# Gathering type-sorted node rows by an inverse index, and spreading the self products over more windows, in a two-layer graph network kernel

## The chip, the core and the metric

One NeuronCore of a Trainium2 chip runs the whole program. The metric is device time of one launch in microseconds (us); lower is better. The engines are TensorE (PE; its weight loads are PEld), VectorE (DVE), ScalarE (ACT), GpSimd (POOL) and SyncE (SP, which here only issues DMAs).

## The reference

Two graph layers on 625 nodes with 512 features and 10,000 edges sorted by destination. With h = relu(layernorm(x)):

- Layer 0: `x = x + relu(h[n] @ W_self[type[n]] + b_self[type[n]] + sum over edges e into n of (h[src[e]] @ W_rel[etype[e]] + b_rel[etype[e]]))`, with three node types and three edge types.
- Layer 1, with h computed anew: `q, k, v = h @ W_qkv.T + b_qkv`, eight heads of 64. Each node attends over its incoming edges, duplicates counted, and `x = x + msg @ W_ff.T + b_ff`.

The change touches only the term h[n] @ W_self[type[n]], and the time at which other work of layer 0 is done.

## The kernel before

Nodes are padded to 640, in NT = 5 tiles of 128 rows.

**Adjacency by windows.** The kernel builds, for each source tile and edge type, a matrix of edge counts adjT (source by destination) in fp16. It goes through NW = 20 windows of 32 destinations. For each window DVE makes a `hot_group`: one tensor_tensor `row_hot` (line 840) and six tensor_scalars `key_hot` (line 833). TensorE multiplies the six pairs into one PSUM bank (`first_chunks`, line 1099), and ACT copies the bank to adjT (`store_window`, line 530). The one-hot buffers are two deep: DVE may make the group of window w + 2 only when TensorE has finished window w.

**Self term.** The rows of one node type must be together to be multiplied by one matrix. DVE computes for each node a place in a list of SORTED = 7 tiles of 128 (`sorted_places`, lines 787 to 796), each tile being of one type. ACT makes the normalised rows in0 (line 546). ACT's queue first fills an HBM tensor `sorted_rows` with zeros (line 538); POOL then scatters in0 to it with five indirect DMAs (line 454), and SP reads the seven tiles back in two transfers (line 374) to `hs`, after which it issues the loads of the two other self matrices and of the relation matrices. Each tile then has a `turn` (four transposes, line 1145, ACT copy) and a `self` unit (four fp32 matmuls of 512 columns, which the trace lists as eight, line 1151, ACT copy, then a DMA to `self_rows`). These 14 units, called the pipe, are put by hand after the chunk matmuls of windows 6 to 12 (`pipe_side`, PIPE_AT = 6): one product per window. POOL later gathers `self_sum` by the same places (line 464).

**Aggregation.** After that come `cnt` units (edge counts by type, line 1192) and `z` units (h aggregated by adjacency, ten matmuls each, line 1206), 8 per relation. The first `cnt` and four `z` units cover the first half of the destinations and are put into windows 15 to 19 (`side`, `first_half`); for that, `all_groups` and `all_chunks` (a fallback for windows with more than six chunks, not taken with these inputs) stand at two points. The rest follows in `schedule`, an ordered list that TensorE, ACT and DVE all walk: the products of each relation (`gemm`, line 1260), logarithms of counts for the attention (`m`), then layer 1.

**Work of the other engines in this stretch.** ACT copies in0 to fp16 (`h16_hi`, after windows 1 to 5) and POOL computes the remainder (line 458). ACT copies relation weights for q = 0 and 1 (`weights_hi`, line 521) right after the last pipe unit; POOL computes their remainders (line 446) and the gathers stand between. Each engine executes in its own program order, so an instruction that waits holds all that is behind it.

Of the kernel before, what the change touches and what calls it, by code (L numbers as in the profile page):

```python
# [36 lines left out]
P = 128  # L37
# [5 lines left out]
def gnn_kernel(nc, x_d, src_d, dst_d, etype_d, ntype_d, wrel_d, brel_d, wself_d, bself_d,  # L43
# [17 lines left out]
    PIPE_AT, PIPE_STEP = 6, 1  # L61
# [10 lines left out]
    with ExitStack() as ctx:  # L72
# [33 lines left out]
        place_u = sb("place_u", [P, NT], U32)  # L106
        bounds = sb("bounds", [1, 3, 32], I32)
# [58 lines left out]
        zero_rows = place("zero_rows", o_ss, [P, D], F32)  # L166
# [18 lines left out]
        sorted_d = nc.dram_tensor("sorted_rows", [SP, D], F32, kind="Internal").ap()  # L185
# [26 lines left out]
        s_half = sem("s_half")  # L212
# [4 lines left out]
        s_zero = sem("s_zero")  # L217
        s_scat = sem("s_scat")
        s_hs = [sem("s_hs0"), sem("s_hs1")]
# [45 lines left out]
        side = {w: [] for w in range(NW)}  # L265
        first_half = [("cnt", 0, 0)] + [("z", 0, dt, 0) for dt in range(KD)]
        for n, u in enumerate(first_half):
            side[NW - len(first_half) + n].append(u)

# [5 lines left out]
        schedule = [u for u in [("cnt", 1, 0)] + z_units(0) + z_units(1) if u not in first_half]  # L275
# [17 lines left out]
        ring = [u for w in range(NW) for u in side[w]] + [u for u in schedule if u[0] not in ("gemm", "sum", "ln")]  # L293
# [9 lines left out]
        pipe_side = {w: [] for w in range(NW)}  # L303
        for n, u in enumerate(pipe):
            pipe_side[PIPE_AT + max(n - 1, 0) * PIPE_STEP // 2].append(u)
# [46 lines left out]
        stored = [NW - len(first_half) + 1, NW]  # L352
# [5 lines left out]
        def _(sp):  # L358
# [46 lines left out]
        def _(pool):  # L405
# [20 lines left out]
            nc.gpsimd.memset(zero_rows[:], 0.0).then_inc(s_fill, 1)  # L426
# [75 lines left out]
        def _(act):  # L502
# [25 lines left out]
            def store_window(w):  # L528
# [8 lines left out]
            act.wait_ge(s_x, 48)  # L537
            act.dma_start(sorted_d.rearrange("(t p) d -> p t d", p=P),
                          zero_rows[:].unsqueeze(1).broadcast_to([P, SORTED, D])).then_inc(s_zero, 16)
# [158 lines left out]
        def _(dve):  # L698
# [98 lines left out]

            def tile_types():
# [15 lines left out]
            def biases():  # L814
                dve.wait_ge(s_prep, 7)
# [31 lines left out]
            def all_groups(half):  # L847

                with dve.If(widest > G):
                    dve.wait_ge(s_adj, stored[half])  # L850
                    for w in range(half * NW // 2, (half + 1) * NW // 2):
# [16 lines left out]
                nc.vector.engine_nop().then_inc(s_half, 1)  # L868
# [96 lines left out]
            factors(0, 0, NT)  # L965
            hot_group(1)
            tile_types()
# [4 lines left out]
            for w in range(NW):  # L972
# [3 lines left out]
                if w + 1 in stored:  # L976
                    all_groups(stored.index(w + 1))
# [10 lines left out]
                for u in side[w]:  # L988
                    unit_part(u)
# [70 lines left out]
        def _(pe):  # L1060
# [50 lines left out]
            ins.then_inc(s_prep, 1)  # L1111

            def all_chunks(half):

                with pe.If(widest > G):
                    pe.wait_ge(s_adj, stored[half])
                    for w in range(half * NW // 2, (half + 1) * NW // 2):
# [14 lines left out]
            def adjacency_of(half):  # L1132

                pe.wait_ge(s_adj, NW // 2 * (half + 1))
                pe.wait_ge(s_half, half + 1)

            def pipe_unit(u):
# [4 lines left out]
                if kind == "turn":  # L1142
                    pe.wait_ge(s_hs[0 if t < 2 else 1], 16)
# [17 lines left out]
            def unit(u):  # L1161
# [9 lines left out]
                elif kind == "cnt":  # L1171
# [3 lines left out]
                    adjacency_of(half)  # L1175
                    if half == 0:
                        pe.wait_ge(s_keys, MASKS)
                        pe.wait_ge(s_fill, FILLS)
# [226 lines left out]
```

## Time and profile before

| what | value |
|---|---|
| median of 3 runs | 335.44 us (334.61 to 335.58) |
| profiled execution, its own time | 335.22 us |
| its span | 333.5 us |
| PE busy | 302.0 us, 91% |
| DVE busy | 201.2 us, 60% |
| ACT busy | 143.0 us, 43% |
| POOL busy | 71.7 us, 22% |
| DMA | 22.29 MB moved |

The span is the time between the first and last record of the profile; the own time of the execution is 1.72 us longer. Busy shares are averages over stages that have different limits. In a timeline row the columns are start in us, length in us, engine, line, operation, output<-input, shape and count; a row of several instructions runs from the first start to the last end. In brackets stands how long the engine had been idle and what released it.

### The profile page before, as it was taken

To read this page: it belongs to the slowest core of one execution; us is meant where nothing else is said; L and a number is where in the kernel's file an instruction comes from. 1 tells how busy PE (TensorE), PEld (TensorE's weight loads), DVE (VectorE), ACT (ScalarE), POOL (GpSimd) and SP (SyncE) were. 2 spreads that over 40 slices of the span, in tenths; PEclk is the share of its full clock that TensorE was granted. 3 is DMA by queue.
4 is the path that set the end of the run, shared out by engine and by line. 5 is a ranking of instruction groups with operands and counts; after the bars stand their busy time and mean duration, and the time that the engine had idled before them with its cause. 6 is when DMAs were issued, how large, how long until landed. Compare 5 with 4: busy or idle time off the path is not lost.

```text
span 333.5 us, 5488 instructions
## 1 busy us (share of the span) xinstructions
PE 302.0 (91%) x2006; PEld 228.6 (69%) x2006; DVE 201.2 (60%) x471; ACT 143.0 (43%) x282; POOL 71.7 (22%) x97
## 2 busy tenths in 40 slices
PE   2757699996699999999999999999799999999994
PEld 2512344442356778868788789999688888888883
DVE  5999944557794324434446962784976556565721
ACT  1155213236032332253342451677876466565721
POOL 6059500005840004470001330320001002020202
PEclk9999789998599999999999999999999999999999
DMA  5852894110740000003520000000000000000000
GB/s 173 281 186 100 267 392 154 38 64 33 253 152 13 2 1 3 2 2 128 149 103 2 0 0 3 0 2 1 0 2 0 34 2 2 32 2 33 1 33 28
DMA packets 10970, 22.29 MB, mean 67 GB/s; under 512 B 950, under 2 KB 966, under 8 KB 10938
## 3 DMA queue, kind: packets, MB, share of 16 engines
q1 hardware_dynamic: 8772, 16.80, 14.5%
q0 software_dynamic: 800, 2.62, 2.2%
q10 hardware_dynamic: 1366, 2.45, 2.1%
q8 instruction: 20, 0.33, 0.4%
q14 instruction: 12, 0.10, 0.1%
HBM read 15.60 MB, written 6.26 MB: 66 GB/s over the span
## 4 chain that ended last, share of the span: by engine, by line
PE 78%; DVE 14%; issue 2%; ACT 2%; DMA 2%; POOL 0%; DVEq 0%
PE banks L1260 13%; PE banks L1246 8%; PE banks L1206 8%; PE banks L1151 8%; PE banks L1349 7%; PE banks L1335 7%; PE banks L1324 7%; DVE key_hot L833 6%; PE banks L1099 6%; PE banks L1369 5%; DVE row_hot L840 3%; PE banks L1192 2%; DMA raw<-in_L_gnn_W_qkv_dram 2%; PE banks L1359 2%; PE banks L1236 1%
## 5 line engine op out<-in xcount | busy, mean ns | idle before, releaser
L1099 PE MATMUL banks<-key_hot,row_hot 128*128 128x480 f16 x120 | 35.8, 438 | 14.7 <-DVE key_hot L833 12.3
L1019 DVE CUSTOM_DVE_ANT_0 s_sb<-banks,mask_add 128x640 f32<-128x640 f32 x40 | 32.6, 822 | 22.2 <-PE banks L1324 22.1
L833 DVE TENSOR_SCALAR key_hot<-iota,picked 128x480 f16<-128x480 f16 x120 | 41.2, 410 | 0.0
L673 ACT ACTIVATE p_sb<-s_sb,neg_max 128x640 f32<-128x640 f32 x40 | 32.9, 823 | 17.3 <-DVE neg_max L1019 17.3
L1099 PEld LDWEIGHTS banks<-key_hot,row_hot 128*128 128x128 f16 x120 | 12.7, 108 | 36.8 <-DVE key_hot L833 15.7
L1206 PE MATMUL banks<-adjT,h 128*128 128x320 f16 x240 | 33.8, 299 | 0.6 <-DVE zT_even L892 0.6
L840 DVE TENSOR_TENSOR row_hot<-iota,picked_row 128x768 f16<-128x768 f16 x20 | 21.9, 1097 | 18.9 <-PE banks L1099 18.9
L1206 PEld LDWEIGHTS banks<-adjT,h 128*128 128x128 f16 x240 | 23.2, 98 | 10.4 <-DVE zT_even L892 1.2
L1335 PE MATMUL banks<-ident,p_sb 128*128 128x128 f32 x200 | 29.6, 275 | 0.2 <-ACT pT L680 0.2
L1260 PE MATMUL banks<-w_hl,zT_even 128*128 128x512 f32 x120 | 29.2, 394 | 0.0
L497 POOL TENSOR_TENSOR msgT<-msg_f,msgT 128x128 fp32r<-128x128 f32 x20 | 8.6, 460 | 95.7 <-ACT msgT L694 95.7
L1324 PE MATMUL banks<-k_hi,q_st 128*128 128x320 f32 x80 | 27.1, 348 | 2.0 <-DVE neg_max L1019 2.0
L1246 PE MATMUL banks<-h2T,wqkvT 128*128 128x320 f32 x192 | 28.3, 309 | 0.0
L1246 PEld LDWEIGHTS banks<-h2T,wqkvT 128*128 128x128 f32 x192 | 28.2, 188 | 0.1
L530 ACT ACTIVATE adjT<-banks 128x480 f16<-128x480 f32 x20 | 11.3, 570 | 37.2 <-PE banks L1099 37.1
L1151 PE MATMUL banks<-w_self,hsT 128*128 x56 | 26.7, 622 | 0.0
L1349 PE MATMUL banks<-pT,v_sb 128*64 128x128 f32 x400 | 26.0, 277 | 0.0
L1335 PEld LDWEIGHTS banks<-ident,p_sb 128*128 128x128 f32 x200 | 23.5, 141 | 3.0 <-issue 1.9
L1260 PEld LDWEIGHTS banks<-w_hl,zT_even 128*128 128x128 f32 x120 | 22.3, 188 | 4.4
L1349 PEld LDWEIGHTS banks<-pT,v_sb 128*64 128x64 f32 x400 | 21.5, 137 | 4.0 <-issue 3.8
L1324 PE MATMUL banks<-k_lo,q_st 128*128 128x320 f32 x80 | 24.0, 309 | 0.0
L446 POOL TENSOR_TENSOR w_hl<-raw,w_hl 128x512 fp32r<-128x512 f32 x12 | 15.0, 1284 | 41.5 <-ACT w_hl L521 41.5
(176 smaller groups left out, 473.3 us busy)
## 6 DMA issues: line engine op xcount, KB each, us to landing
w_self<-in_L_gnn_W_self_dram SPq DMA_DIRECT2D x3, 1024.0 KB, 9.4
raw<-in_L_gnn_W_rel_dram SPq DMA_DIRECT2D x3, 1024.0 KB, 14.6
raw<-in_L_gnn_W_qkv_dram SPq DMA_DIRECT2D x3, 1024.0 KB, 5.2
sorted_rows<-zero_rows ACTq DMA_DIRECT2D x1, 1792.0 KB, 10.9
self_rows<-hs SPq DMA_DIRECT2D x7, 256.0 KB, 2.0
hs<-sorted_rows SPq DMA_DIRECT2D x1, 1280.0 KB, 7.2
xs<-in_x_dram SPq DMA_DIRECT2D x1, 1024.0 KB
raw<-in_L_gnn_W_ff_dram SPq DMA_DIRECT2D x1, 1024.0 KB, 5.4
```

What stands on the lines that cost most here:

```text
L673: nc.scalar.activation(p_sb[:, n % NPR, :], s_sb[:, n % NS, :], ACT.Exp, scale=-1.0, bias=neg_max[:, it, h:h + 1], accum_out=denom[:, it, ...
L833: return nc.vector.tensor_scalar(to_key, iota[:], float(KEYS * w), key, ALU.add, ALU.is_equal)
L840: nc.vector.tensor_tensor(row_hot[:, par], iota[:, 0:P].unsqueeze(1).broadcast_to([P, G, P]), picked_row[:, w * G:(w + 1) * G].unsqueeze(2 ...
L1019: nc.vector.tensor_tensor_reduce(s_sb[:, n % NS, :].rearrange("p (a j) -> p a j", a=2), banks[:, c:c + 2, 0:HALF], mask_add[:, it, :].rear ...
L1099: mm(banks[:, w % 2, 0:KEYS], row_hot[:, w % 2, k, :], key_hot[:, w % 2, k, :], start=(k == 0), stop=True, skip_group_check=True).then_inc ...
L1151: ins = mm(pipe_bank(u), hsT[:, t % 4, kt, :], w_self[:, bass.ds(offsets[t] + kt * D, D)], start=(kt == 0), stop=(kt == KD - 1))
L1206: ins = mm(b[:, 0:HALF], h16[:, p, jt, feats], adj[:, jt, r, cols], start=(start and n == 0), stop=(stop and n == len(pick) - 1), skip_gro ...
L1246: ins = mm(b[:, 0:HALF], wqkvT[:, pw, kt, o:o + P], h2T[:, ph, kt, half * HALF:(half + 1) * HALF], start=(n == 0), stop=(n == 3 * KD - 1))
L1260: ins = mm(to, lhs[:, pl, kt, it * P:(it + 1) * P], weights[:, pw, kt, c0:c0 + cn], start=(start and n == 0), stop=(n == 3 * KD - 1), skip ...
L1324: ins = mm(banks[:, 2 * (n % 2) + half, 0:HALF], q_st[:, h, it * P:(it + 1) * P], k[:, h, cols], start=(p == 0), stop=(p == 1))
L1335: ins = nc.tensor.transpose(banks[:, 5 + n % 2, i * P:(i + 1) * P], p_sb[:, h % NPR, jt * P:(jt + 1) * P], ident[:])
L1349: ins = mm(banks[64 * hh:64 * hh + 64, 4, a * P:(a + 1) * P], v_sb[:, jt, h * DK:(h + 1) * DK], pT[:, s, :], start=(jt == 0), stop=(jt == ...
```

## The change

Three things change. (1) The zero fill, the scatter and the read back go. SP stores the five tiles of in0 in node order (`rows`), between the loads of self matrices 1 and 2. DVE makes five 128x896 one-hots of the places, TensorE multiplies them with the node numbers in 35 matmuls of one column, DVE turns the result into `node_u`, and POOL gathers the seven tiles into `hs`, with a semaphore for each. (2) The pipe starts at window 3, and product t stands at window 3 + 16t // 7, so at windows 3, 5, 7, 9, 12, 14 and 16. The first `cnt` and four `z` units leave the windows and go to the front of `schedule`; the fallback stands once, after window 19. (3) `h16_hi` moves to windows 9 to 13, and `weights_hi(0)` and `weights_hi(1)` go behind the windows and in front of relation 1's z units.

```diff
-    PIPE_AT, PIPE_STEP = 6, 1
+    PIPE_FROM, PIPE_OVER = 3, 16
-        schedule = [u for u in [("cnt", 1, 0)] + z_units(0) + z_units(1) if u not in first_half]
+        schedule = [("cnt", 0, 0), ("cnt", 1, 0)] + z_units(0) + z_units(1)
-        pipe = [("turn", 0), ("turn", 1)]
+        pipe_side = {w: [] for w in range(NW)}
+        pipe_side[PIPE_FROM] += [("turn", 0), ("turn", 1)]
         for t in range(SORTED):
-            pipe += [("self", t)] + [("turn", t + 2)] * (t + 2 < SORTED)
+            pipe_side[PIPE_FROM + t * PIPE_OVER // SORTED] += [("self", t)] + [("turn", t + 2)] * (t + 2 < SORTED)
...
             self_weights(0)
-            sp.wait_ge(s_scat, 16 * NT)
-            for half, (t0, t1) in enumerate(((0, 2), (2, SORTED))):
-                sp.dma_start(hs[:, t0:t1, :], sorted_d[t0 * P:t1 * P, :].rearrange("(t p) d -> p t d", p=P)
-                             ).then_inc(s_hs[half], 16)
             self_weights(1)
+            for it in range(NT):
+                sp.wait_ge(s_y0, it + 1)
+                sp.dma_start(rows_d[it * P:(it + 1) * P, :], in0[:, it, :]).then_inc(s_rows, 16)
             self_weights(2)
...
-            pool.wait_ge(s_place, 1)
-            pool.wait_ge(s_zero, 16)
-            for it in range(NT):
-                pool.wait_ge(s_y0, it + 1)
-                nc.gpsimd.indirect_dma_start(sorted_d, bass.IndirectOffsetOnAxis(ap=place_u[:, it:it + 1], axis=0),
-                                             in0[:, it, :], None).then_inc(s_scat, 16)
+            nc.gpsimd.iota(slot_iota[:], [[1, SP]], base=0, channel_multiplier=0,
+                           allow_small_or_imprecise_dtypes=True).then_inc(s_fill, 1)
+            pool.wait_ge(s_node, 1)
+            pool.wait_ge(s_rows, 16 * NT)
+            for t in range(SORTED):
+                nc.gpsimd.indirect_dma_start(hs[:, t, :], None, rows_d,
+                                             bass.IndirectOffsetOnAxis(ap=node_u[:, t:t + 1], axis=0)).then_inc(s_hs[t], 16)
...
-            act.dma_start(sorted_d.rearrange("(t p) d -> p t d", p=P),
-                          zero_rows[:].unsqueeze(1).broadcast_to([P, SORTED, D])).then_inc(s_zero, 16)
...
-                        if u == pipe[-1]:
-                            weights_hi(0)
-                            weights_hi(1)
-                    for u in side[w - 1]:
-                        unit_part(u)
                     store_window(w)
-                if 1 <= w < 1 + NT:
-                    h16_hi(w - 1)
-            for u in side[NW - 1]:
-                unit_part(u)
+                if 9 <= w < 9 + NT:
+                    h16_hi(w - 9)
+            weights_hi(0)
             for u in schedule:
-                if u == ("z", 2, 0, 0):
-                    weights_hi(2)
+                if u in (("z", 1, 0, 0), ("z", 2, 0, 0)):
+                    weights_hi(u[1])
...
+            def place_one_hots():
+                dve.wait_ge(s_fill, FILLS + 1)
+                for it in range(NT):
+                    nc.vector.tensor_scalar(place_hot[:, it, :], slot_iota[:], place_n[:, it:it + 1], None,
+                                            ALU.is_equal).then_inc(s_inv, 1)
+
+            def nodes_of_slots():
+                dve.wait_ge(s_prep, 7)
+                nodes = banks[:, 4, 460:460 + SORTED]
+                nc.vector.tensor_scalar(node_u[:], nodes, -1.0, 0.0, ALU.add, ALU.max).then_inc(s_node, 1)
...
             factors(0, 0, NT)
+            place_one_hots()
             hot_group(1)
+            nodes_of_slots()
             tile_types()
...
+            pe.wait_ge(s_inv, NT)
+            for t in range(SORTED):
+                for it in range(NT):
+                    ins = mm(banks[:, 4, 460 + t:461 + t], place_hot[:, it, t * P:(t + 1) * P], node_id[:, it:it + 1],
+                             start=(t == 0 and it == 0), stop=True, skip_group_check=True)
+            ins.then_inc(s_prep, 1)
...
-                    pe.wait_ge(s_hs[0 if t < 2 else 1], 16)
+                    pe.wait_ge(s_hs[t], 16)
```

The 35 matmuls stand on TensorE after the rank matmuls of line 1108 and before the chunks of window 1. TensorE also waits for s_node at window 2.

## Rows read from the trace of the kernel before

**Rows 1.** Busy time by stretch: us, each engine's busy (instructions), granted clock, DMA share, GB/s
```profile
0.00:38.00 38.00, 20.92 (x69) 10.13 (x69) 33.40 (x104) 11.83 (x20) 21.71 (x39) 0.98 0.56 187
38.00:77.00 39.00, 38.90 (x128) 19.20 (x129) 21.01 (x64) 11.93 (x22) 0.00 (x0) 0.93 0.46 172
77.00:103.00 26.00, 19.98 (x97) 10.33 (x95) 21.79 (x40) 8.56 (x12) 15.64 (x13) 0.80 0.40 144
```

**Rows 2.** Timeline, TensorE and DVE in the windows of the self products
```profile
66.34 1.38 PE L1099 MATMUL banks<-key_hot,row_hot 128*128 128x480 f16 x6
...
71.43 1.38 PE L1099 MATMUL banks<-key_hot,row_hot 128*128 128x480 f16 x6
...
72.85 0.96 DVE L840 TENSOR_TENSOR row_hot<-iota,picked_row 128x768 f16<-128x768 f16 x1 [2.60 <-PE banks L1099]
...
76.08 2.59 PE L1099 MATMUL banks<-key_hot,row_hot 128*128 128x480 f16 x12
```

**Rows 3.** Timeline, the windows after the last product
```profile
78.37 5.66 DVE L833 TENSOR_SCALAR key_hot<-iota,picked 128x480 f16<-128x480 f16 x6
78.75 5.13 POOL L446 TENSOR_TENSOR w_hl<-raw,w_hl 128x512 fp32r<-128x512 f32 x4 [40.88 <-ACT w_hl L521]
...
87.16 4.21 PE L1192 MATMUL banks<-adjT,sel 128*70 128x320 f16 x15
...
92.72 3.89 DVE L840 TENSOR_TENSOR row_hot<-iota,picked_row 128x768 f16<-128x768 f16 x1 [0.30 <-PE banks L1099]
```

**Rows 4.** Busy time by stretch, the lowest clock in those windows
```profile
84.00:88.00 4.00, 1.72 (x8) 0.99 (x9) 4.00 (x12) 0.57 (x1) 3.35 (x3) 0.50 0.60 207
```

**Rows 5.** Timeline, the second cnt unit and twelve z units
```profile
103.20 2.20 PE L1192 MATMUL banks<-adjT,sel 128*70 128x320 f16 x15
105.24 16.46 PE L1206 MATMUL banks<-adjT,h 128*128 128x320 f16 x120
```

**Rows 6.** Timeline, ACT and DVE before window 2
```profile
17.91 2.91 ACT L546 ACTIVATE in<-xs,shift,rstd 128x512 f32<-128x512 f32 x4
...
19.46 0.21 DVE L799 TENSOR_SCALAR tile_off<-tile_iota,type_base 1x8 f32<-1x8 f32 x1
...
21.32 0.93 DVE L840 TENSOR_TENSOR row_hot<-iota,picked_row 128x768 f16<-128x768 f16 x1
...
23.71 0.94 DVE L840 TENSOR_TENSOR row_hot<-iota,picked_row 128x768 f16<-128x768 f16 x1
```

**Rows 7.** Timeline, small matmuls with a new stationary operand each
```profile
13.02 2.25 PEld L1108 LDWEIGHTS banks<-type_mask,ones 128*128 128x128 f32 x10
...
124.54 1.01 PE L1223 MATMUL banks<-ident,adjT 128*128 128x128 f16 x15
```

**Rows 8.** Lines 454 and 464: ns min/median/max, first and last start; landing of 464
```profile
L454 POOL DMA_INDIRECT sorted_rows<-in,place_u x5: 960/1175/5195, 20.2 to 31.1; - x5
...
L464 POOL DMA_INDIRECT self_sum<-self_rows,place_u x5: 946/960/1716, 84.0 to 89.9; - x5
...
DMA to landing us min/median/max: 4.1/4.4/6.0
```

**Rows 9.** The longest scatter, in the POOL timeline
```profile
24.21 5.20 POOL L454 DMA_INDIRECT sorted_rows<-in,place_u  x1 [0.30 <-issue]
```

**Rows 10.** Timeline, POOL and DVE at window 6, and the first self product
```profile
32.06 5.82 POOL L458 TENSOR_TENSOR h<-in,h 128x512 f16<-128x512 f32 x5
...
32.18 6.09 DVE L833 TENSOR_SCALAR key_hot<-iota,picked 128x480 f16<-128x480 f16 x6
...
40.79 5.10 PE L1151 MATMUL banks<-w_self,hsT 128*128 x8
```

**Rows 11.** Timeline, POOL weight remainders beside a z unit's DVE part
```profile
144.57 4.95 POOL L446 TENSOR_TENSOR w_hl<-raw,w_hl 128x512 fp32r<-128x512 f32 x4 [0.57 <-ACT w_hl L521]
147.58 0.49 DVE L892 TENSOR_TENSOR zT_even<-banks,zT_even 128x320 fp32r<-128x320 f32 x1 [1.37 <-ACT zT_even L573]
```

**Rows 12.** DMA issues: KB each, median us to landing
```profile
self_rows<-hs SPq DMA_DIRECT2D x7, 256.0 KB, 2.0
```

More of the change, by code:

```diff
@@ L106, in gnn_kernel @@
         place_u = sb("place_u", [P, NT], U32)
+        node_u = sb("node_u", [P, SORTED], U32)
         bounds = sb("bounds", [1, 3, 32], I32)
@@ L165, in gnn_kernel @@
         place_n = place("place_n", o_r4 + 61472, [P, NT], F32)
-        zero_rows = place("zero_rows", o_ss, [P, D], F32)
+        slot_iota = place("slot_iota", o_r4 + 61760, [P, SP], F16)
+        node_id = place("node_id", o_r4 + 63552, [P, NT], F16)
+        place_hot = place("place_hot", o_z0 + 10240, [P, NT, SP], F16)
         mlog = place("mlog", o_r4 + 43136, [P, 2, 512], F32)
@@ L183, in gnn_kernel @@
         msgT = place("msgT", o_r4 + 27136, [P, 2, 2, KD, P], F32R)
-        sorted_d = nc.dram_tensor("sorted_rows", [SP, D], F32, kind="Internal").ap()
+        rows_d = nc.dram_tensor("rows", [NP, D], F32, kind="Internal").ap()
         self_d = nc.dram_tensor("self_rows", [SP, D], F32, kind="Internal").ap()
@@ L216, in gnn_kernel @@
         s_wself = [sem(f"s_wself{t}") for t in range(T)]
-        s_zero = sem("s_zero")
-        s_scat = sem("s_scat")
-        s_hs = [sem("s_hs0"), sem("s_hs1")]
+        s_inv = sem("s_inv")
+        s_node = sem("s_node")
+        s_rows = sem("s_rows")
+        s_hs = [sem(f"s_hs{t}") for t in range(SORTED)]
         s_pipe = sem("s_pipe")
@@ L262, in gnn_kernel @@
         s_out = [sem("s_out0"), sem("s_out1")]
[L265 to L268, printed above, removed]
         def z_units(r):
             return [("z", r, dt, half) for dt in range(KD) for half in range(2)]
-        schedule = [u for u in [("cnt", 1, 0)] + z_units(0) + z_units(1) if u not in first_half]
+        schedule = [("cnt", 0, 0), ("cnt", 1, 0)] + z_units(0) + z_units(1)
         for it in range(NT):
@@ L292, in gnn_kernel @@
         schedule += [("q", a, half) for a in range(KD) for half in range(2)]
-        ring = [u for w in range(NW) for u in side[w]] + [u for u in schedule if u[0] not in ("gemm", "sum", "ln")]
+        ring = [u for u in schedule if u[0] not in ("gemm", "sum", "ln")]
         number = {u: n for n, u in enumerate(ring)}
@@ L297, in bank @@
             return banks[:, 5 + number[u] % 3, :]
-        pipe = [("turn", 0), ("turn", 1)]
+        pipe_side = {w: [] for w in range(NW)}
+        pipe_side[PIPE_FROM] += [("turn", 0), ("turn", 1)]
         for t in range(SORTED):
-            pipe += [("self", t)] + [("turn", t + 2)] * (t + 2 < SORTED)
+            pipe_side[PIPE_FROM + t * PIPE_OVER // SORTED] += [("self", t)] + [("turn", t + 2)] * (t + 2 < SORTED)
+        pipe = [u for w in range(NW) for u in pipe_side[w]]
         pipe_no = {u: n for n, u in enumerate(pipe)}
-        pipe_side = {w: [] for w in range(NW)}
-        for n, u in enumerate(pipe):
-            pipe_side[PIPE_AT + max(n - 1, 0) * PIPE_STEP // 2].append(u)
         def pipe_bank(u):
@@ L845, in hot_group, with all_groups @@
                     key_one_hot(key_hot[:, par, k, :], picked[:, 1, n:n + 1], w).then_inc(s_hot, 1)
-            def all_groups(half):
+            def all_groups():
                 with dve.If(widest > G):
-                    dve.wait_ge(s_adj, stored[half])
-                    for w in range(half * NW // 2, (half + 1) * NW // 2):
+                    dve.wait_ge(s_adj, NW)
+                    for w in range(NW):
                         lo = dve.value_load(bounds[0:1, 0, w:w + 1], min_val=0, max_val=EC)
@@ L987, in _ @@
                                             bhl[BG:BG + R + T, :].bitcast(F32), ALU.subtract).then_inc(s_blo, 1)
-                for u in side[w]:
-                    unit_part(u)
+            all_groups()
             for u in schedule:
@@ L1111, in _, with all_chunks @@
             ins.then_inc(s_prep, 1)
-            def all_chunks(half):
+            pe.wait_ge(s_inv, NT)
[4 more added lines that the diff above has]
+            ins.then_inc(s_prep, 1)
+            def all_chunks():
                 with pe.If(widest > G):
-                    pe.wait_ge(s_adj, stored[half])
-                    for w in range(half * NW // 2, (half + 1) * NW // 2):
+                    pe.wait_ge(s_adj, NW)
+                    for w in range(NW):
                         count = pe.value_load(bounds[0:1, 2, w:w + 1], min_val=1, max_val=EC)
@@ L1174, in unit @@
                     cols = slice(half * HALF, (half + 1) * HALF)
-                    adjacency_of(half)
                     if half == 0:
+                        pe.wait_ge(s_adj, NW)
+                        pe.wait_ge(s_whole, 1)
                         pe.wait_ge(s_keys, MASKS)
@@ L1274, in _ @@
                         skip_runtime_bounds_check_because="the vector engine worked them out")
-                if w + 1 in stored:
-                    all_chunks(stored.index(w + 1))
                 for u in pipe_side[w]:
                     pipe_unit(u)
-                for u in side[w]:
-                    unit(u)
                 if w == 6:
@@ L1284, in _ @@
                                         ).then_inc(s_prep, 1)
+            all_chunks()
             for u in schedule:
```

18 lines of the change are left out of this document (6 added, 12 removed).

## The prediction, made before the changed kernel was run

> **What bounds the kernel now.** I read the busy time by stretch first. Up to 38 us DVE is busy 33.4 of 38 us and TensorE only 20.9; from 38 to 77 us TensorE is busy all the time (38.9 of 39) and DVE 21.0; from 77 to 103 us neither is full, 20.0 and 21.8 of 26 us [rows 1]. So the 20 windows are bound by DVE, then by TensorE, then by turns by each. The timelines say why. In the middle part a window lasts 5.09 us (chunk matmuls start at 66.34 and 71.43), and DVE stands idle for 2.60 us of it until TensorE is done with a buffer [rows 2]. A DVE group alone needs 2.39 us (row_hot starts at 21.32 and 23.71) [rows 6]. Six chunk matmuls alone add 1.22 us on TensorE (12 of them last 2.59 us and six 1.38), and a window with a product but no turn lasts 4.65 us (71.43 to 76.08) [rows 2]. Hence a product costs 4.65 - 1.22 = 3.43 us and its turn 5.09 - 4.65 = 0.44 us.
>
> Twenty groups are 47.8 us of DVE work, and the chunks, products and turns are 24.4 + 24.0 + 3.1 = 51.5 us of TensorE work at full speed. Run beside each other they would need little over 50 us. In the trace they go from about 18 us (group 1) to 103 us, with 9 to 10 us of cnt and z units among them. The losses besides the unequal mixing are four. Six key_hots took 6.09 us where POOL's subtractions ran at 32 us [rows 10]; in a free group 2.39 us less row_hot's 0.93 is left for them, about 1.6 us with the overlap of neighbours [rows 6]. Six took 5.66 us and one row_hot 3.89 us beside POOL's weight remainders [rows 3]. The first cnt unit took 4.21 us at a granted clock of about 0.5, the lower level of 1.2 GHz, against 2.20 us for the second [rows 3 to 5]. These are 4.5 + 4.0 + 2.9 + 2.0 = 13.4 us, almost all on the path.
>
> **The change, as a new walk through the windows.** The terms below are not differences but a clock time for each step, since many of them overlap.
>
> *The index.* DVE's five 128x896 one-hots are not in the trace. A key_hot of 480 elements adds about 0.27 us (1.6 / 6) [rows 6]. No more than in proportion, 0.50 us, and no less than the same, 0.27: 1.3 to 2.5 us in all. I take 2.0 (0.4 each), since a fixed part must be in 0.27. Group 1, which started at 17.07 (21.32 less 1.86 of small operations, less 2.39) [rows 6], ends at 21.5. TensorE's 35 one-column matmuls run beside it, from 19.1. Their price is that of loading a new 128x128 operand: 0.07 us in the 15 fp16 matmuls of 1.01 us at full clock, 0.225 us in fp32 [rows 7], so 2.4 to 7.9 us. I take twice the pitch that lies between 0.85 and 1.01 us for 15 (0.057), for the lower clock: 0.113 x 35 = 4.0 us, to 23.1. DVE waits for them in front of tile_types, with groups 2 and later queued behind the wait. So node_u is ready at 23.3, and the small operations of 1.86 us [rows 6] put group 2 at 25.2 instead of 21.32: **+3.9 us** at once, visible on the path. Group 3 ends at 30.0, 4 at 32.4, 5 at 34.8.
>
> *Stores and gathers.* in0 is complete at 20.8 [rows 6]; SP has nothing before the stores but two weight loads issued by 9 us, and a 256 KB store lands in 2.0 us [rows 12], so `rows` is there at about 23.3, beside node_u. This edit takes no time of its own: the index ends as late. POOL then issues seven gathers. Undisturbed one takes 0.96 us and 0.3 us between [rows 9], median landing 4.4 us; under DVE's groups five scatters went from 20.2 to 32.0, so 2.36 us each [rows 8], the longest 5.20 [rows 9]. The bounds for a gather are thus 1.26 and 5.5 us. The first falls beside DVE's small operations and is issued at 24.7. With 2.4 us for the second it is issued at 27.4, with 5.5 at 30.2; landing 4.4 us gives 31.8 to 34.6. I take 33.6. The third lands before 38 and is needed only after the first product.
>
> *A rule about this.* Rows 9 show a scatter held for 5.20 us while DVE made groups back to back, and rows 8 that others got through in about 1 us. The Trainium skill ("SBUF — State Buffer", section "SBUF: two separate sides") says that a DVE instruction in a two-port mode locks GpSimd out, so that it cannot write the descriptors of its DMAs. Taken strictly, gathers advance only when DVE stands still, which would be after group 5. The rows support it only in part; what it would cost is worked out as rival B.
>
> *Window 3.* The chunks of windows 2 and 3 at the lower level end at about 31.4; turn 0 follows to 32.2, turn 1 waits for its gather and ends at 34.0, and the first product takes 5.10 us as it did before at the lower level [rows 10]: 39.1, and with turn 2 39.5. Window 4's chunks end at 40.8 and, as group 5 is long ready, window 5's at 42.0.
>
> *Steady windows.* A window with a product and one without are 5.09 + 1.22 = 6.31 us of TensorE against 4.78 us of DVE. So window 7 ends at 48.3 and 9 at 54.6. From 9 to 12 there are three windows: DVE's two groups after window 10 give 5.09 + 2.39 + 0.3 = 7.8 us. In this stretch POOL's five h16 remainders now run, 5.82 / 5 = 1.16 us each, one per window [rows 10]. Spread out, most fall into DVE's slack; I charge 1.0 here and 0.7 in 12 to 14, between 0 and 4.5 (what they cost before). Window 12 ends at 63.4 and 14 at 70.4 (6.31 + 0.7). The products of windows 14 and 16 have no turn behind them: 16 ends at 76.3 (4.65 + 1.22) and 17 at 80.9. Then DVE decides, with group 19 made after that: 83.6.
>
> *After the windows.* Both cnt units and all z units follow: 0.3 + 2.4 + 2.2 us, and 16 z at 16.46 / 12 = 1.37 us, 21.9 us [rows 5]. This is 26.8 us, to **110.4 us**. Before, the z units ended at 121.7 (105.24 + 16.46) [rows 5]. The gain is 11.3 us. weights_hi(0) runs on ACT beside the cnt units, where ACT has no copies to make; weights_hi(1) delays an ACT copy by some 1 us, within the three banks of the ring. POOL's remainders now lie beside z units; their DVE part took 0.49 us beside just such POOL work [rows 11], so I charge nothing. Without that cover, four POOL operations would hold DVE for 4 us each time, as in rows 3. Behind this point the order of work is unchanged.
>
> **Sum.** 335.2 - 11.3 = 323.9 us against the profiled execution's own time, which lies 0.2 us under the median shown, so I keep 323.9.
>
> **Rivals.**
> A. *Nothing delays window 3.* The second gather lands in time and TensorE is at its upper level, since it has been nearly continuously busy from 19 us. Then turn 1 saves 1.4 us and the product 1.7, and with 1 us less for the index it is about 4 us better: 319.9 us. For it: the granted clock up to 38 us is 0.98 on average [rows 1]. Against: the first product took 5.10 us all the same [rows 10].
> B. *The gathers starve.* DVE goes back to back from 25.2 to 34.8, as it did when one scatter took 5.20 us. Gathers 1 and 2 are issued after 35 us, gather 1 lands at about 40.5, and window 4 ends near 47.8 instead of 40.8: 7 us less gain, 330.9 us. Against it: half of the scatters amid groups took no more than 1.18 us [rows 8]. By the rule of the Trainium skill's page this is what happens.
> C. *Slower: TensorE's clock does not hold in the thinned windows.* Where products stood in every window the clock was at its full level; where DVE paced the windows it fell, to 0.5 at 84 to 88 us [rows 4]. Now DVE paces windows 10 to 12 and 16 to 19. If the clock falls there and stays low through the cnt units, then work worth 16.8 us from 12 to 16 (three products, a turn and five sets of chunks) doubles, of which TensorE's own waits hide about 4, so that 13 us are added: about 336.9 us. It turns the result to slower from the point where more than 11.3 us of full-speed work runs at the lower level. Against it: the idle times now are 1 to 2 us at a time, and windows with products have no gap.
> D. *No change.* B's 7 us and a lower level at one place alone, for some 4 us of work, give 11 together: 335 us, within 0.3% (1 us, about what a measurement of this kernel can tell from no change).
>
> **Chances.** Forecast 0.50 (its own range 321.9 to 326.5), A 0.16, B 0.24, C 0.05, D and its like 0.05. The predicted time is the forecast's, 323.9. The range goes from 319.7, A, to 331.5, B with half a microsecond more. Faster by over 0.3%: 0.90; same 0.04; slower 0.06.
>
> **What would show it.** Right: group 2 starts near 25 us; the 35 matmuls last 4 us; the first product starts near 34 and lasts 5.1 us; products at windows 5, 7, 9 leave DVE idle for 1.5 us per pair; no key_hot group of over 5 us; window 19's chunks end at 83 to 85; z ends near 110. Wrong: gathers of over 4 us each before the first product (B), or lower-level rows after 45 us (C). If the windows end at 84 but the time doesn't fall by 11 us, something in layer 1 moved, which I excluded.

## The result, and the profile after

The changed kernel takes 330.83 us (329.81 to 330.99, 4 runs) beside 335.51 us before; the ratio is 0.9855 (95% interval 0.9824 to 0.9887). So it is faster, by 4.7 us and not by 11.3. Its profiled execution took 330.99 us (span 329.2), against 335.22. The z units of relations 0 and 1 end at 117.4 us instead of 121.7 [rows 5], and 4.2 of these 4.3 us are left at the end: behind this point nothing changed, as forecast. All that has to be explained lies in the windows and, for 1.4 us, in the cnt and z units right behind them.

The index first. Timeline of DVE and of TensorE in the changed kernel, before window 2:

```profile
21.12 0.15 DVE L797 TENSOR_SCALAR node_u<-banks 128x7 uint32<-128x7 f32 x1
...
23.05 0.94 DVE L841 TENSOR_TENSOR row_hot<-iota,picked_row 128x768 f16<-128x768 f16 x1
```

```profile
18.86 1.09 PE L1115 MATMUL banks<-node_id,place_hot 128*128 128x1 f16 x35 [3.66 <-DVE place_hot L790]
19.98 2.58 PE L1099 MATMUL banks<-key_hot,row_hot 128*128 128x480 f16 x6
```

The 35 matmuls last 1.09 us, and node_u is there at 21.3, not 23.3; group 2 starts at 23.05 instead of 21.32 [rows 6]. But the index is no longer what ends last. The chain of waits, in order of time (start, us, what):

```profile
20.69 4.22 DMA rows<-in
...
25.77 8.74 DMA hs<-rows,node_u
...
34.56 1.11 PE banks L1146 x4
...
36.93 5.10 PE banks L1152 x8
...
57.77 3.43 PE banks L1152 x8
...
63.85 2.83 DVE key_hot L834 x4
...
67.61 5.20 PE banks L1152 x8
...
89.19 0.58 ACT adjT L528
```

The first two rows are the stores of `rows` (the last is issued at 20.69 and landed at 24.9) and the first gather with its transfer (8.74 us). TensorE waits for them in front of turn 0 until 34.5. The row at 63.85 is DVE held at six key_hots, and the one after it a product that took 5.20 us where 3.43 is normal. DMA issues by line, with KB each and median us to landing, say the same of the first part:

```profile
rows<-in SPq DMA_DIRECT2D x5, 256.0 KB, 4.0
...
hs<-rows,node_u POOLq DMA_INDIRECT x7, 6.4
```

A store lands in 4.0 us where rows 12 had 2.0, a gather in 6.4 where rows 8 had 4.4. DVE's timeline shows what follows for it:

```profile
43.72 0.96 DVE L841 TENSOR_TENSOR row_hot<-iota,picked_row 128x768 f16<-128x768 f16 x1 [10.68 <-PE banks L1099]
...
63.76 3.41 DVE L834 TENSOR_SCALAR key_hot<-iota,picked 128x480 f16<-128x480 f16 x6
...
68.79 2.58 DVE L834 TENSOR_SCALAR key_hot<-iota,picked 128x480 f16<-128x480 f16 x6
...
75.38 2.51 DVE L834 TENSOR_SCALAR key_hot<-iota,picked 128x480 f16<-128x480 f16 x6
```

DVE is idle for 10.68 us, since both buffers are full while TensorE stands at window 3; later three of its groups are held by POOL's h16 remainders (key_hots of 3.41, 2.58 and 2.51 us instead of 1.60). The busy time by stretch (columns as in rows 1) has the low granted clock of the product at window 12, which lasts 5.37 us in the timeline:

```profile
68.00:72.00 4.00, 4.00 (x7) 1.58 (x6) 4.00 (x8) 0.74 (x2) 1.15 (x1) 0.64 0.02 6
```

The first product lasts 5.31 us in the timeline, but the granted clock of 36.7 to 42 us is given as 1.00. That it ran in part at the lower level is read from its length (3.60 us for the others), here and in the runs below, and not from the clock column.

### The profile page after: what moved, and what is told of

Same layout as the page of the kernel before. It is cut to its first block, busy times and chain, and to the rows that moved or that the text cites. A ratio compares the mean times of both kernels' runs of the same rounds, so it can differ in the third digit from the quotient of the medians.

```text
span 329.2 us, 5541 instructions
## 1 busy us (share of the span) xinstructions
PE 300.2 (91%) x2041; PEld 229.0 (70%) x2041; DVE 195.8 (59%) x477; ACT 143.1 (43%) x282; POOL 70.5 (21%) x100
## 4 chain that ended last, share of the span: by engine, by line
PE 80%; DVE 7%; DMA 6%; ACT 3%; issue 2%; POOL 1%; ACTq 0%; DVEq 0%; POOLq 0%
PE banks L1261 13%; PE banks L1247 9%; PE banks L1207 9%; PE banks L1152 8%; PE banks L1348 7%; PE banks L1334 7%; PE banks L1323 7%; PE banks L1099 6%; PE banks L1368 5%; DMA hs<-rows,node_u 3%; DMA raw<-in_L_gnn_W_qkv_dram 2%; PE banks L1358 2%; PE banks L1237 1%; PE banks L1194 1%; PE banks L1146 1%
## 5 line engine op out<-in xcount | busy, mean ns | idle before, releaser
L1099 PE MATMUL banks<-key_hot,row_hot 128*128 128x480 f16 x120 | 32.0, 413 | 5.5 <-DVE key_hot L834 5.4
L834 DVE TENSOR_SCALAR key_hot<-iota,picked 128x480 f16<-128x480 f16 x120 | 36.0, 366 | 0.0
L841 DVE TENSOR_TENSOR row_hot<-iota,picked_row 128x768 f16<-128x768 f16 x20 | 19.9, 994 | 15.9 <-PE banks L1099 15.7
L1152 PE MATMUL banks<-w_self,hsT 128*128 x56 | 28.7, 660 | 0.0
L528 ACT ACTIVATE adjT<-banks 128x480 f16<-128x480 f32 x20 | 11.4, 570 | 26.2 <-PE banks L1099 25.8
L669 ACT ACTIVATE pT<-banks 128x512 f32<-128x512 f32 x25 | 14.6, 586 | 14.5 <-PE banks L1334 14.5
```

What stands on the lines that cost most here:

```text
L834: return nc.vector.tensor_scalar(to_key, iota[:], float(KEYS * w), key, ALU.add, ALU.is_equal)
L841: nc.vector.tensor_tensor(row_hot[:, par], iota[:, 0:P].unsqueeze(1).broadcast_to([P, G, P]), picked_row[:, w * G:(w + 1) * G].unsqueeze(2 ...
L1099: mm(banks[:, w % 2, 0:KEYS], row_hot[:, w % 2, k, :], key_hot[:, w % 2, k, :], start=(k == 0), stop=True, skip_group_check=True).then_inc ...
L1152: ins = mm(pipe_bank(u), hsT[:, t % 4, kt, :], w_self[:, bass.ds(offsets[t] + kt * D, D)], start=(kt == 0), stop=(kt == KD - 1))
```

## The experiments

All times are medians; ratios are to the kernel before, on the same chip. The changed kernel gave 330.8 and, in a later set, 329.5 us, so a gain against it is known to about 1.3 us. Differences to the changed kernel are given against both sets where that matters.

| run | us | ratio (95%) |
|---|---|---|
| changed kernel | 330.8 | 0.9855 (0.9824 to 0.9887) |
| the same again (e11) | 329.5 | 0.9845 (0.9819 to 0.9871) |
| e1 weight loads after the third tile | 327.2 | 0.9770 (0.9744 to 0.9796) |
| e2 h16 copies at windows 1 to 3 | 327.0 | 0.9762 (0.9719 to 0.9805) |
| e9 bias broadcasts first | 328.4 | 0.9825 (0.9789 to 0.9861) |
| e12 these three together | 323.0 | 0.9665 (0.9628 to 0.9702) |
| e7 products from window 4 | 326.5 | 0.9770 (0.9740 to 0.9801) |
| e3 products from window 5 | 321.4 | 0.9591 (0.9566 to 0.9615) |
| e5 from window 5, one in each window | 329.2 | 0.9860 (0.9820 to 0.9900) |
| e8 e3 with e1, e9 and spaced h16 copies | 319.8 | 0.9554 (0.9531 to 0.9577) |
| e4 part 1 of the change alone | 332.5 | 0.9924 (0.9902 to 0.9947) |
| e6 parts 2 and 3 alone | 328.7 | 324.1 to 333.1, no ratio given |
| e6b the same again | 330.8 | 325.6 to 332.7, no ratio given |
| e10 e3 with scatters | 321.6 | 319.5 to 327.4, no ratio given |
| e14 e3 with scatters and a pause of DVE | 321.2 | 0.9595 (0.9571 to 0.9619) |

What one kernel's executions differ in is seen in the changed kernel itself. The profile of e11 (327.45 us) has nearly the same wait of TensorE (4.15 us) and POOL's remainders at the same place, but both slow products are shorter than in the profile above (5.31 and 5.37 us):

```profile
36.70 4.13 PE L1152 MATMUL banks<-w_self,hsT 128*128 x8
...
66.24 3.68 PE L1152 MATMUL banks<-w_self,hsT 128*128 x8
```

These are 2.9 of the 3.5 us between the two executions. What decides it, no run here shows.

**e1_loads_late.** The late tiles: whose fault?

```diff
+            sp.wait_ge(s_hs[2], 16)
             self_weights(2)
```

> SP waits for the third gathered tile before it issues the loads of self matrix 2 and of relation matrices 0 and 1 (3 MB). Theory T (the missing gain has two causes: gathered rows that land late behind these loads, and POOL's h16 remainders in windows paced by DVE): landing of the gathers falls from 6.4 us to about 4.4, the first product starts at 34 to 35 us instead of 36.7, the time falls by about 2 us to 329. Rival P (the gathers are late because DVE's groups hold up their issue): issue and landing stay, first product at 36.7 us, time 331 as after.

Its DMA issues, and TensorE's timeline:

```profile
hs<-rows,node_u POOLq DMA_INDIRECT x7, 4.5
```

```profile
32.18 1.97 PE L1147 MATMUL banks<-ident,hs 128*128 128x128 f32 x8 [1.79 <-DMA hs<-rows,node_u]
34.18 4.62 PE L1153 MATMUL banks<-w_self,hsT 128*128 x8
```

Landing falls to 4.5 us, the issues keep their lengths (2.16, 2.09, 1.46, then 0.95 us), and TensorE's wait falls from 4.21 to 1.79 us. Theory T holds for this cause, P does not for the landing. The gain is 3.7 us (2.3 against the later set) where 2 were expected; in the profiles the first product starts 2.5 us earlier. The rest of the difference to the first profile (4.62 instead of 5.31 us for this product, 3.68 instead of 5.37 for the one at window 12) came in e11 without this edit.

**e2_h16_early.** POOL's remainders.

```diff
-                if 9 <= w < 9 + NT:
-                    h16_hi(w - 9)
+                for it in ((), (0, 1), (2, 3), (4,))[w] if w < 4 else ():
+                    h16_hi(it)
```

> ACT's fp16 copies of in0 go to windows 1 to 3 instead of 9 to 13, so that POOL's remainders follow the gathers at 37 to 43 us, where DVE is idle. Theory T: no key_hot group over 2 us in windows 9 to 14, the product of window 12 back from 5.37 to 3.6 us, windows 9 to 14 about 3 to 4 us shorter, time 327. Rival C (spread windows let TensorE's clock fall by themselves): the clock falls in windows 10 to 12 all the same and the time falls by less than 1.5 us.

Timeline of POOL, and of TensorE at window 12:

```profile
37.21 5.60 POOL L456 TENSOR_TENSOR h<-in,h 128x512 f16<-128x512 f32 x5
```

```profile
63.57 1.56 PE L1099 MATMUL banks<-key_hot,row_hot 128*128 128x480 f16 x6 [0.18 <-DVE key_hot L834]
64.97 3.68 PE L1152 MATMUL banks<-w_self,hsT 128*128 x8
```

The five remainders lie in DVE's idle time, no group is held, and the product of window 12 takes 3.68 us: 3.8 us gained (2.5 against the later set), near T's 3 to 4. Windows thinned out by themselves did not let the clock fall. In e1 and in e11 the same remainders held DVE just as long and the product of window 12 took 3.68 us as well. So the clock's fall does not have to follow, and of the 3.8 us the 1.7 of this product are not shown to be the edit's.

**e9_bias_first.** Why a store lands late.

```diff
+            act.dma_start(bv_rows[:], bqkv_d[2 * D:3 * D].partition_broadcast(P)).then_inc(s_bias, 16)
+            act.dma_start(bff_rows[:], bff_d.partition_broadcast(P)).then_inc(s_bias, 16)
             def weights_hi(q):
...
                 rows0(it)
-            act.dma_start(bv_rows[:], bqkv_d[2 * D:3 * D].partition_broadcast(P)).then_inc(s_bias, 16)
-            act.dma_start(bff_rows[:], bff_d.partition_broadcast(P)).then_inc(s_bias, 16)
```

> The two broadcast loads bv_rows and bff_rows (256 KB each) go from 17 us, just ahead of the stores of rows, to the start of ACT's queue. Theory B (these two make a store land in 4.1 us instead of 2.0): stores land in under 3 us, POOL's first gather is issued at about 24 us instead of 25.8, the first product starts 1 to 2 us earlier, time 329.5. Rival W (the stores wait for the weight loads or for nothing that moves): landing 4 us, gather at 25.8, time 331.

```profile
rows<-in SPq DMA_DIRECT2D x5, 256.0 KB, 2.1
...
hs<-rows,node_u POOLq DMA_INDIRECT x7, 6.8
```

```profile
23.93 1.12 POOL L452 DMA_INDIRECT hs<-rows,node_u  x1 [17.19 <-DMA rows<-in]
...
27.63 0.95 POOL L452 DMA_INDIRECT hs<-rows,node_u  x1 [0.30 <-issue]
```

A store lands in 2.1 us and the first gather is issued at 23.93 instead of 25.77. Theory B holds. The first product starts 1.7 us earlier (35.01), but lasts 5.54 us. The gathers land in 6.8 us; that they do so because they are now issued nearer to the 3 MB of weights is argued from e1, not tested here. The time is 2.4 us lower (1.1 against the later set).

**e12_three_terms.** The three edits together, products still from window 3.

> The changed kernel, products from window 3, with the edits of e1_loads_late, e2_h16_early and e9_bias_first together, which restore three sizes that the forecast assumed (a store lands in 2.0 us, a gather in 4.4, POOL's remainders cost little). Theory T3 (the forecast failed by these sizes and not in its walk): first product at 32 to 33 us, window 19's chunks at about 83, time 323 to 325, the forecast's 323.9. Rival K (window 3 is a bad place in itself, since TensorE has no chunk work behind it while DVE fills both buffers): 326 or more, as the best of the three alone.

```profile
32.25 3.66 PE L1154 MATMUL banks<-w_self,hsT 128*128 x8
...
86.86 21.90 PE L1209 MATMUL banks<-adjT,h 128*128 128x320 f16 x160
```

The kernel takes 323.0 us; the forecast was 323.9, and rival K's 326 is out. But the steps of the walk did not come out with the sum. Window 5 ends at 38.8 us, 3.2 before the forecast's 42.0: the first product starts at 32.25 instead of 34.0 and lasts 3.66 us instead of 5.10. The z units start at 86.9, only 1.6 before the forecast's 88.5. One thing lost in between is in DVE's timeline:

```profile
37.60 4.78 DVE L843 TENSOR_TENSOR row_hot<-iota,picked_row 128x768 f16<-128x768 f16 x1 [4.55 <-PE banks L1101]
```

TensorE now frees the buffer earlier, so POOL's remainders (35.95 to 41.56) no longer lie in DVE's idle time; this row_hot takes 4.78 us instead of 0.95, and the product of window 7 starts about 1.7 us late. So the third size was moved, not restored, and part of the agreement with 323.9 is luck.

**e3_from5, e7_from4.** Not to wait at all.

```diff
-    PIPE_FROM, PIPE_OVER = 3, 16
+    PIPE_FROM, PIPE_OVER = 5, 14
```

(e7: `4, 15`.)

> Products at windows 5, 7, 9, 11, 13, 15 and 17 instead of 3 to 16. Theory T: TensorE goes on with the chunks of windows 4 and 5 while the tiles are in flight, its 4.2 us wait in front of the first turn goes, and the time falls by 2 to 3 us, to 328. Rival P: without an idle DVE the gathers are issued at over 4 us each, the first product starts after 41 us, the time is 331 or more.

> Products at windows 4, 6, 8, 10, 12, 14 and 16. Theory T2: the chunks of window 4 end at about 33.5 us, turn 0 waits for 1 us and turn 1 for another, and the time lies between after and e3_from5, nearer to the latter: 324 us. Rival C2 (the difference of 9.4 us between after and e3_from5 is mostly TensorE's clock, which fell in the wait): with the wait cut to 2 us the clock stays up and all of it comes back, 321.5 us.

TensorE's timeline in e3, then in e7:

```profile
27.81 6.32 PE L1099 MATMUL banks<-key_hot,row_hot 128*128 128x480 f16 x18 [0.84 <-DVE key_hot L834]
...
35.53 0.66 PE L1146 MATMUL banks<-ident,hs 128*128 128x128 f32 x4 [0.97 <-DMA hs<-rows,node_u]
36.02 3.60 PE L1152 MATMUL banks<-w_self,hsT 128*128 x8
...
85.78 21.90 PE L1207 MATMUL banks<-adjT,h 128*128 128x320 f16 x160
```

```profile
33.29 0.66 PE L1146 MATMUL banks<-ident,hs 128*128 128x128 f32 x4 [0.54 <-DMA hs<-rows,node_u]
35.74 0.90 PE L1146 MATMUL banks<-ident,hs 128*128 128x128 f32 x4 [1.80 <-DMA hs<-rows,node_u]
36.44 5.09 PE L1152 MATMUL banks<-w_self,hsT 128*128 x8
```

In e3 the first product starts at 36.0 us, only 0.7 us before that of the changed kernel, but with two more windows done, and it lasts 3.60 us instead of 5.31. The z units of e3 start at 85.8 instead of 95.0. The gain is 9.4 us (8.1 against the later set) and not the expected 3. Time in which TensorE waits at window 3 is lost on DVE as well, whose two buffers are full; in e3 DVE made groups 6 and 7 meanwhile.

The profiles allow a split of the 9.7 us by the end of the z units. With window 5, the first product and its turn done, e3 is 5.0 us ahead (39.9 against 44.9): 2.4 for the chunks of two windows, 1.7 for the product's length, the rest for the earlier start. Another 3.7 arise up to window 19 and 1.0 behind it. There e3 differs in more than its start: its products stand in every second window up to 17, none of its products took over 3.68 us, and POOL's remainders, which stretched two groups of key_hots to 3.41 us, held TensorE up by only about 0.7 us. So not all of the 9.4 us is the wait at window 3.

Rival P is out: e3's gathers took 2.19, 2.09 and 1.43 us and then 0.94 to 1.23, though DVE worked on. At window 4 the waits are 0.54 and 1.80 us, but the first product still takes 5.09 us. C2's 321.5 us is refuted: with the waits cut to 2.3 us the product is as slow as before. By the lengths above, the clock is 1.7 us of the difference at the first product and up to 1.7 at window 12, so not most of 9.4. 326.5 us is less near to e3 than I expected.

**e5_from5_dense.** What the spreading itself is worth (`5, 7`).

> Products start at window 5, as in e3_from5, but stand in every window, 5 to 11, instead of every second one. Theory T2 (the start at window 3 cost most of the missing gain, the spreading is worth as much as DVE's idle time in windows bound by TensorE): windows 5 to 11 take 5.1 us each with 2.6 us of DVE idle, then windows 12 to 19 are paced by DVE at 2.4 us with nothing else on TensorE, so 20 - 6 = about 7 us are lost against e3_from5 and the time is 328. Rival N (only the later start matters): 321 to 322 as e3_from5.

```profile
35.93 3.60 PE L1152 MATMUL banks<-w_self,hsT 128*128 x8
...
73.80 0.38 PE L1099 MATMUL banks<-key_hot,row_hot 128*128 128x480 f16 x1 [0.75 <-DVE key_hot L834]
...
83.85 1.56 PE L1099 MATMUL banks<-key_hot,row_hot 128*128 128x480 f16 x6 [0.83 <-DVE key_hot L834]
86.24 1.56 PE L1099 MATMUL banks<-key_hot,row_hot 128*128 128x480 f16 x6 [0.83 <-DVE key_hot L834]
```

Started as e3, it is 7.8 us slower, T2's 7 us and not N's nothing. After the last product TensorE waits for DVE: within a window whose key_hots POOL's remainders hold (0.75 us at 73.80), and for 0.83 us in front of each of the last ones, so that a window lasts 2.39 us (83.85 to 86.24). From 76 to 80 us the granted clock was 0.57, which is part of the 7.8. So starting late enough and spreading are both needed.

**e4_gather_only.** Part 1 alone, in the kernel before.

> The kernel before with part 1 of the change alone (stores, index, seven gathers); products in windows 6 to 12, half units, h16 copies and weight copies stay where they were. Theory T: the tiles are there at about 36 us instead of 38, POOL's h16 remainders fall into the windows bound by TensorE instead of window 6, so the first product starts at 37 to 38 instead of 40.8 and the time is 332 to 333. Rival S (the gain is all in the spreading): the later group 2 eats what the gathers save, time 335.

```profile
37.75 3.70 PE L1173 MATMUL banks<-w_self,hsT 128*128 x8 [0.47 <-ACT hsT L603]
```

```profile
36.99 7.42 DVE L847 TENSOR_SCALAR key_hot<-iota,picked 128x480 f16<-128x480 f16 x6
...
75.84 5.66 DVE L847 TENSOR_SCALAR key_hot<-iota,picked 128x480 f16<-128x480 f16 x6
```

The first product starts at 37.8 instead of 40.8 and lasts 3.70 us instead of 5.10: 2.5 us gained, as expected. But POOL's remainders still stop DVE, now in group 7 (six key_hots in 7.42 us), and the weights stop it at 75.8 as in rows 3.

**e6_scatter_spread, e6b, e10, e14: what the gathers are worth.** These keep the zero fill, the scatters and the read back, with parts 2 and 3 of the change.

> Parts 2 and 3 of the change alone: products from window 3, spread, with the zero fill, scatter and read back of the kernel before. Theory T2: the tiles land at 38 us or later, so that TensorE waits at window 3 for 7 us or more instead of 4.2; part 3 takes POOL's remainders out of window 6 and the weights out of the windows; 332 to 334 us. Rival S (parts 2 and 3 carry the gain by themselves): 331 as after.

> The kernel of e6_scatter_spread again, since its four executions lay between 324.1 and 333.1 us. If they spread alike again, the time hangs on how long the scatters are held (one took 6.85 us in that profile); T2 expects a median of 329 to 333, not under that of e11_change_again by more than 2 us; rival S expects it 2 us under it.

> The changed kernel itself, beside the others: 330.8 us, for the comparison with e6b_scatter_spread on one chip.

> e3_from5 with the zero fill, scatter and read back in place of stores, index and gathers; so against e3_from5 it shows what part 1 is worth when the products start at window 5. Theory T2: the tiles land at 38.5 us, window 5 ends at 33, TensorE waits 5 us, the clock falls, and the time is 326 to 327, so part 1 is worth about 5 us. Rival S: 322, part 1 is worth nothing as it costs DVE 2 us for the index.

The executions of these kernels lie far apart: 324.1, 328.2, 329.2 and 333.1 us for e6, 325.6 to 332.7 in six executions of e6b, and 319.5, 319.9, 323.2 and 327.4 us for e10. By its median e6b (330.8) is not under e11 (329.5) on the same chip, so rival S, which wanted it 2 us lower, is out. The profiles caught both ends. POOL's timeline in e6 (333.1 us), e6b (325.6) and e10 (327.4):

```profile
22.58 6.85 POOL L447 DMA_INDIRECT sorted_rows<-in,place_u  x1 [0.31 <-issue]
```

```profile
21.18 0.97 POOL L447 DMA_INDIRECT sorted_rows<-in,place_u  x1 [0.30 <-ACT in L539]
22.46 0.96 POOL L447 DMA_INDIRECT sorted_rows<-in,place_u  x1 [0.30 <-issue]
```

```profile
22.53 7.07 POOL L447 DMA_INDIRECT sorted_rows<-in,place_u  x1 [0.30 <-issue]
```

And what TensorE waited for in e6 and in e6b, in front of the first turn:

```profile
38.80 1.97 PE L1124 MATMUL banks<-ident,hs 128*128 128x128 f32 x8 [10.19 <-DMA hs<-sorted_rows]
```

```profile
31.60 1.97 PE L1124 MATMUL banks<-ident,hs 128*128 128x128 f32 x8 [2.23 <-DMA hs<-sorted_rows]
```

One scatter held for 6.85 us goes with tiles at 38.8 us, none held with tiles at 31.6. It ends at 29.4 us, as the held one of rows 9 did (24.21 + 5.20), soon after DVE's first wait for a buffer, which in the trace of before came at 28.6 us. In e6b DVE's groups 2 and 3 took 0.15 to 0.2 us longer each and the scatters went through; in e6 it ran without a break. Which of the two is the cause, the profiles don't show. For this the last kernel makes DVE stand still while the scatters are issued:

```diff
                 if w == 2:
+                    dve.wait_ge(s_pause, 32)
...
-                                             in0[:, it, :], None).then_inc(s_scat, 16)
+                                             in0[:, it, :], None).then_inc(s_pause if it < 2 else s_scat, 16)
```

> e10_scatter_from5 with DVE waiting in front of group 2 until the first two scatters have landed, so that DVE stands still for about 3 us while POOL issues the second to fourth scatter. Theory H (a scatter is held by DVE's groups made back to back until DVE's first pause): the executions come within 1.5 us of each other, no scatter takes over 2.5 us in the profile, and the time is 321 to 324 us, since the pause costs DVE about 3 us. Rival Q (the hold comes from the DMA queues, where 2.8 MB of zeros and weights are under way until 19 us): scatters of 5 us or more again, and executions 5 us or more apart.

```profile
23.87 0.96 DVE L831 TENSOR_TENSOR row_hot<-iota,picked_row 128x768 f16<-128x768 f16 x1 [2.24 <-DMA sorted_rows<-in,place_u]
```

```profile
22.40 0.96 POOL L449 DMA_INDIRECT sorted_rows<-in,place_u  x1 [0.30 <-issue]
...
24.92 1.00 POOL L449 DMA_INDIRECT sorted_rows<-in,place_u  x1 [0.30 <-issue]
```

No scatter is held, and four executions lie between 321.03 and 321.68 us. All three marks of theory H came out, and none of rival Q's. The last scatter (24.92) went through beside running groups, so a busy DVE alone does not hold one. With products from window 5, scatters and a pause cost the same as stores, index and gathers (321.4), and e10's two fastest executions, without a pause, 1.5 to 1.9 us less: there part 1 is worth evenness, not time. In the kernel before, it was worth 2.5 us (e4). At window 3 the tiles of unheld scatters came 3 us before the gathered ones. My expectation for e10 (326 to 327, part 1 worth 5 us) took a held scatter for the rule, as that one trace of before had shown it.

**e8_best.** e3 with e1 and e9, and one h16 copy in windows 6, 8, 10, 12 and 14.

> Four edits together: products from window 5 in every second window, the weight loads after the third gathered tile, the two bias broadcasts at the start of ACT's queue, and one h16 copy in each window without a product from 6 to 14. Theory T2: what is left in e3_from5 is 1 us of wait at the second tile and 0.7 us around POOL's remainders, so 320 us (319.5 to 320.7). Rival O (the edits take each other's place, since the first product of e3_from5 already starts when window 5 ends): 321.4, no difference.

```profile
35.10 3.69 PE L1154 MATMUL banks<-w_self,hsT 128*128 x8 [0.47 <-issue]
...
84.12 21.90 PE L1209 MATMUL banks<-adjT,h 128*128 128x320 f16 x160
```

319.75 us, 4.5% under the kernel before and 1.6 us under e3; T2 holds. From 33.6 us TensorE has hardly a gap up to the end of the windows. e12 with nearly the same edits, but products from window 3, takes 3.3 us more. With window 5, the first product and its turn done, the two stand level (39.2 us here, 38.8 in e12), so a start at window 3 costs nothing there once the tiles come early. e12 loses behind that point: at window 7, as shown above, and at windows 12 and 19, where the chunks of three windows in a row (10 to 12, 17 to 19) let DVE set the pace.

## Why the prediction was wrong

The direction was right, and so was where the gain lies: the 4.3 us are there when the z units end, no group was held by weight remainders, layer 1 did not move. The size was off by more than a factor of two, because three steps of the walk were mis-sized: the landing of the stores, the landing of the gathers, and what POOL's remainders cost. Forecast and trace, in us from the start:

| step | forecast | measured |
|---|---|---|
| node_u ready | 23.3 | 21.3 |
| first gather's issue starts | 23.4 (24.7 less 1.26) | 25.8 |
| first product starts, its length | 34.0, 5.10 | 36.7, 5.31 |
| window 5 ends | 42.0 | 44.9 |
| window 9 ends | 54.6 | 57.8 |
| window 12, 14 ends | 63.4, 70.4 | 67.6, 75.7 |
| window 19 ends | 83.6 | 89.2 |
| z units | 88.5 to 110.4 | 95.0 to 117.4 |

- *"This edit takes no time of its own: the index ends as late"* failed, twice over. The index came 2.0 us early (its matmuls were bounded at 2.4 us from below by matmuls of 128 columns, and one-column matmuls took 1.09), and the stores 2 us late. The 2.0 us of rows 12 is a median of seven stores, five of them issued after 55 us, where the queues moved about 52 GB/s, little more than these stores themselves; the stores of `rows` had two broadcasts just ahead (e9).
- *Landing 4.4 us, "I take 33.6"* failed likewise: 6.4 us, since SP issues 3 MB of weights in front of the gathers (e1). I had listed SP's queue and looked only at what stands before the stores. Together 2.9 us by window 5, and 0.3 more by window 9.
- *The remainders, "I charge 1.0 here and 0.7"*: 1.0 too little between windows 9 and 12, and another 1.1 to window 14, where the clock fell for one product (5.37 us). e2 gives back 3.8 us (2.5 against the later set).
- *After the windows*: window 19 itself ended another 0.3 us late. Then 0.71 us for ACT's copy of window 19 and small gaps between the two cnt units, 1.0 us by the start of the z units. Within them 0.4 us were lost to an ACT copy that came about 1.9 us late at 103.9 us, for a reason that the trace does not show; in e11, the same kernel, the 160 matmuls run through in 21.90 us. weights_hi(1) was hidden, as forecast.

These are 2.9 + 0.3 + 1.0 + 1.1 + 0.3 + 1.0 + 0.4 = 7.0 us, the difference at 117.4. They are those of one execution at the slow end; in e11's profile the z units end at 114.1, 3.7 us behind the forecast, mostly since the two products at 36.7 and 66.2 us were shorter. e12 supports that these sizes failed: with the stores and gathers early and the remainders elsewhere it takes 323.0 us against 323.9. It does not prove the walk, whose steps it passes by up to 3.2 us before it loses part of that again. What the walk did not ask is whether window 3 and the uneven spacing were good choices: it took a wait of TensorE at its length, though DVE with full buffers pays it again, and it let DVE set the pace at windows 12 and 19, behind the chunks of three windows in a row. e3, which changes both, is 9.4 us faster; with tiles and broadcasts early as well, the difference is 3.3 us (e12 against e8).

Rival B's number, 330.9, came out, but not by its mechanism: gathers were issued in 2.3 us, not held until DVE's pause, and e3 with a busy DVE issued them alike. So it is luck that the time lies within the stated range, whose upper part stood there for B. Rival C's clock fall came for a single product, and not in e11. D and A did not occur.

## What to carry to other kernels

Price a DMA by a row with the same company, not by the nearest row of the same size: list what every queue issues in the 5 us before and after it. Put work that waits for a transfer behind the point where the transfer has surely landed, above all when the waiting engine feeds a partner with two buffers, since both then stop. And when a kernel's executions spread, as those of e6, e10 and, by 3.5 us, the changed kernel do, ask for the profile at either end before pricing what one of them showed.

## What was unexpected of the hardware

- A 256 KB store landed in 4.0 us with two 256 KB broadcasts issued just ahead on another queue, and in 2.1 us without them.
- An indirect DMA's issue takes 0.95 us alone. Under back-to-back DVE groups, the first two gathers took 2.1 to 2.3 us and ended just after the start of a row_hot (28.04 and 30.43 us, against starts at 27.84 and 30.39), one per group. In e9, under groups as dense, three in a row took 0.95 to 1.01 us. A scatter went through in 0.96 us or was held for 6.85 to 7.07 us, until about DVE's first pause. The Trainium skill ("SBUF — State Buffer", section "SBUF: two separate sides") says that DVE in a two-port mode keeps GpSimd from writing descriptors. The scatters agree with it (7.07 us, and none held with DVE paused), but a busy DVE was not enough: after 32 us in e3 the gathers took 0.94 to 1.23 us beside groups with key_hots of 1.77 us, and in e6b, without a pause, no scatter took over 1.18 us. Why gathers and scatters differ stays open.
- 35 matmuls of one column, each with a new 128x128 fp16 operand, took 1.09 us, 31 ns each, while the six chunk matmuls right behind them took 2.58 us, where six take 1.38 us later on.
